# Rotary attention: statistics, root and normalizing of the next batch one quad of heads earlier; chunk attention: rows normalized by GpSimd

## The reference, cut to what matters

```python
x = x + _L0_attn_a_ref(_layernorm(x, axis=-1), Wq, Wk, Wv)          # "chunk attention"
x = x + _L0_ffn_ref(_layernorm(x, axis=-1), ...)                    # expert ffn
x = x + _L0_attn_b_ref(_layernorm(x, axis=-1), Wq, Wk, Wv, Wo, bo)  # "rotary attention"
...                                                                 # five more sublayers
```

## Time and profile before

| | |
|---|---|
| median of 3 runs | 4226.66 us (4223.68 to 4236.27) |
| the profiled execution | 4221.0 us, of which the span is 4219.3 us |
| TensorE busy | 3577.8 us (85%) |
| VectorE busy | 2677.2 us (63%) |
| ScalarE busy | 2302.2 us (55%) |
| GpSimd busy | 1990.1 us (47%) |
| mean granted TensorE clock | 0.907 of full speed |
| 500 to 600 us (chunk attention) | PE 95.71, DVE 86.40, ACT 70.01, POOL 25.44 of 100; granted clock 1.00 |
| 1600 to 2600 us (rotary attention) | PE 970.01, DVE 639.13, ACT 588.33, POOL 671.17 of 1000; granted clock 0.99 |

### The profile page before, as it was taken

One profiled execution on the slowest core, in us unless ns is written; L12 is line 12 of the kernel. 1 busy time (PEld: TensorE's weight loads), 2 busy tenths in 40 slices (PEclk: granted clock), 3 DMA queues, 4 the chain that ended last, 5 costly groups with the idle time before them and its releaser, 6 DMA issues. The chain is left out here.

```text
span 4219.3 us, 89135 instructions
## 1 busy us (share of the span) xinstructions
PE 3577.8 (85%) x31200; PEld 2222.9 (53%) x31295; DVE 2677.2 (63%) x5798; ACT 2302.2 (55%) x5504; POOL 1990.1 (47%) x1991
## 2 busy tenths in 40 slices
PE   5999999966858999999999999996857776787768
PEld 1333333325854556656565565555755665575546
DVE  6888888855445666666666666655455665555465
ACT  2766776753324556555555555553325553575367
POOL 2222222217435666666666666757431111565175
PEclk8999999985878999999999999995878997897879
DMA  5333333301551112111111111122542222110001
GB/s 98 58 58 58 58 58 58 58 28 59 184 160 45 47 41 50 42 44 48 42 47 44 41 47 45 44 54 60 182 145 63 68 65 50 33 62 6 1 1 41
DMA packets 418236, 252.24 MB, mean 60 GB/s; under 512 B 251186, under 2 KB 344354, under 8 KB 416642
## 3 DMA queue, kind: packets, MB, share of 16 engines
q1 hardware_dynamic: 409156, 228.56, 23.3%
q0 software_dynamic: 8640, 17.97, 1.3%
HBM read 75.12 MB, written 41.75 MB: 28 GB/s over the span
## 5 line engine op out<-in xcount | busy, mean ns | idle before, releaser
L2496 POOL TENSOR_TENSOR ra_prob<-ra_prob,ra_inverse 128x256 f32<-128x256 f32 (+3 forms) x512 | 630.6, 1253 | 472.0 <-DVE ra_inverse L2719 472.0
L2655 ACT ACTIVATE ra_prob<-ra_ps_s,ra_low 128x128 f32<-128x128 f32 (+3 forms) x1024 | 535.0, 530 | 320.6 <-DVE ra_low L2700 320.2
L2311 DVE TENSOR_REDUCE ca_mx<-ca_ps_s 128x2 f32<-128x1024 f32 x512 | 600.6, 1211 | 112.7 <-PE ca_ps_s L2172 112.4
L2237 ACT ACTIVATE ca_pT<-ca_ps_p 128x512 f32<-128x512 f32 x1024 | 548.8, 603 | 219.6 <-PE ca_ps_p L2182 195.0
L2700 DVE TENSOR_REDUCE ra_low<-ra_ps_s 128x2 f32<-128x256 f32 (+3 forms) x512 | 406.4, 815 | 77.5 <-PE ra_ps_s L2599 76.2
L2172 PE MATMUL ca_ps_s<-ca_kst,ca_qst 128*128 128x512 bf16 x991 | 381.2, 390 | 49.9 <-DVE ca_mx L2311 28.2
L2707 DVE TENSOR_TENSOR ra_prod<-ra_ps_r,ra_cos 128x512 f32<-128x512 f32 x256 | 176.6, 690 | 313.4 <-PE ra_ps_r L2561 265.2
L2182 PE MATMUL ca_ps_p<-ca_qst,ca_kst 128*128 128x512 bf16 x962 | 362.5, 382 | 4.9 <-ACT ca_pT L2237 4.5
L2536 PE MATMUL ra_ps_t<-ident,ra_prob 128*128 128x128 f32 x2560 | 352.9, 276 | 3.0 <-ACT ra_probT L2661 1.8
L2661 ACT COPY ra_probT<-ra_ps_t 128x512 f32<-128x512 f32 x384 | 226.4, 590 | 235.0 <-PE ra_ps_t L2536 234.9
L2489 POOL TENSOR_TENSOR ra_rot<-ra_prod 128x512 f32<-128x512 f32 x256 | 320.9, 1275 | 62.9 <-DVE ra_prod L2708 62.7
(11 more groups left out here) (413 smaller groups left out, 7162.2 us busy)
## 6 DMA issues: line engine op xcount, KB each, us to landing
moe_w_own<-moe_w1T SPq DMA_DIRECT2D x142, 256.0 KB
ra_qz<-ra_rot SPq DMA_DIRECT2D x512, 64.0 KB, 2.0
ra_kz<-ra_rot SPq DMA_DIRECT2D x512, 64.0 KB, 2.0
ca_kst<-ca_bounce SPq DMA_DIRECT2D x256, 64.0 KB
ca_bounce<-ca_thirds SPq DMA_DIRECT2D x192, 64.0 KB, 2.9
ca_qst<-ca_bounce SPq DMA_DIRECT2D x64, 192.0 KB
moe_hs<-moe_rows SPq DMA_DIRECT2D x142, 66.0 KB
moe_raw<-in_L_ffn_W SPq DMA_DIRECT2D x32, 256.0 KB, 3.2
```

Source lines behind the costliest of these rows:

```text
L2237: nc.scalar.activation(pT[:, (NS * hp + u) % PRING, :], ps_p[n % NP][:], ACT.Exp).then_inc(sg["drained"], 1)
L2311: nc.vector.tensor_reduce(mx[:, hm % 2, 2 * j:2 * j + 2], ps_s[m % 2][:].rearrange("p (b k) -> p b k", b=2), AX.X, ALU.max)\
L2496: nc.gpsimd.tensor_tensor(at, at, inverse[:, n % PROB, 2 * tile:2 * tile + 2].unsqueeze(2).broadcast_to([P, 2, keys]), ALU.mult)\
L2655: nc.scalar.activation(prob[:, n % PROB, tile, head, 0:keys], part(n, tile)[:, head, :], ACT.Exp, bias=low[:, n % PROB, at:at + 1], scale= ...
```

## The change

In chunk attention GpSimd applies the row norm to the two tiles itself, right behind the two roots, and VectorE's application at j = 12 is gone. VectorE's statistics now wait for the tile normalized two before, since the mean's buffer has two places. In rotary attention a new index `coming` marks the quad k = 4b - 2; statistics (slots 0 to 3) and root (slot 3) stand there, and the normalizing stands in its slot 7. The bias goes to slot 3 of quad 4b - 1; the transposes stay in slot 7 of that quad. The loop starts one iteration earlier (k = -2), in which only the norm of batch 0 stands.

```diff
@@ chunk_attention, gpsimd @@
                     if h is not None:
                         for c in range(2):
                             norm.rstd(pool, 2 * h + c, c)
+                        for c in range(2):
+                            t = 2 * h + c
+                            pool.wait_ge(norm.rstd_done, t + 1)
+                            nc.gpsimd.tensor_scalar(tile_of(xn, t), tile_of(X, t), norm.mv[:, c, 0:1], norm.rs[:, c:c + 1], ALU.subtract, ALU.mult)\
+                                .then_inc(sg["x_normed"], 1)
                     if hp is not None:
                         outputs(hp, 0)
@@ chunk_attention, vector @@
                         for c in range(2):
+                            wait(dve, sg["x_normed"], 2 * h + c - 1)
                             norm.stats(dve, 2 * h + c, c, tile_of(X, 2 * h + c))
-                    if j == 12:
-                        for c in range(2):
-                            dve.wait_ge(norm.rstd_done, 2 * h + c + 1)
-                            norm.apply(tile_of(xn, 2 * h + c), tile_of(X, 2 * h + c), c).then_inc(sg["x_normed"], 1)
@@ rope_attention, slots @@
-            for k in range(-1, QUADS + OUT):
+            for k in range(-2, QUADS + OUT):
...
-                    batch = (k + 1) // NQ if (k + 1) % NQ == 0 and k + 1 < QUADS else None
-                    body(j, t, s, front, score, value, out, batch)
+                    batch = (k + 1) // NQ if (k + 1) % NQ == 0 and 0 <= k + 1 < QUADS else None
+                    coming = (k + 2) // NQ if (k + 2) % NQ == 0 and k + 2 < QUADS else None
+                    body(j, t, s, front, score, value, out, batch, coming)
@@ rope_attention, gpsimd @@
+                    if coming is not None and j == 3:
+                        pool.wait_ge(sg["var_done"], coming + 1)
+                        nc.gpsimd.tensor_tensor(rs[:], var[:], core.minus_half[:, 0:TC], ALU.pow).then_inc(sg["rs_done"], 1)
+                    if coming is not None and j == 7:
+                        pool.wait_ge(sg["rs_done"], coming + 1)
+                        wait(pool, sg["x_turned"], coming)
+                        for c in range(TC):
+                            nc.gpsimd.tensor_scalar(xn[:, c, :], X[:, coming * TC + c, :], mv[:, c, 0:1], rs[:, c:c + 1], ALU.subtract, ALU.mult)\
+                                .then_inc(sg["x_normed"], 1)
                     if batch is not None and j == 3:
-                        pool.wait_ge(sg["var_done"], batch + 1)
-                        nc.gpsimd.tensor_tensor(rs[:], var[:], core.minus_half[:, 0:TC], ALU.pow).then_inc(sg["rs_done"], 1)
-                    if batch is not None and j == 5:
-                        ...
-                    if batch is not None and j == 7:
                         pool.wait_ge(sg["x_normed"], TC * (batch + 1))
                         xb = X[:, batch * TC:(batch + 1) * TC, :]
                         nc.gpsimd.tensor_tensor(xb, xb, bias[:].unsqueeze(1).broadcast_to([P, TC, D]), ALU.add).then_inc(sg["x_biased"], 1)
@@ rope_attention, vector @@
-                    if batch is not None and j < TC:
+                    if coming is not None and j < TC:
                         if j == 0:
-                            wait(dve, sg["x_normed"], TC * batch)
+                            wait(dve, sg["x_normed"], TC * coming)
...
```

More of the change, by code:

```diff
@@ L2462, in move, with body @@
                             sp.dma_start(to[at:at + HALF, n % RING, :], rot[h * HALF:(h + 1) * HALF, front % 2, o, x, :]).then_inc(qk_ready[n % RING], 16)
-                def body(j, t, s, front, score, value, out, batch):
+                def body(j, t, s, front, score, value, out, batch, coming):
                     if front is None or j not in (3, 5):
@@ L2507, in body @@
                         divide(score, 0)
-                    if batch is not None and j == 3:
-                        pool.wait_ge(sg["var_done"], batch + 1)
-                        nc.gpsimd.tensor_tensor(rs[:], var[:], core.minus_half[:, 0:TC], ALU.pow).then_inc(sg["rs_done"], 1)
-                    if batch is not None and j == 5:
[L2512 to L2516, removed]
-                    if batch is not None and j == 7:
+                    if coming is not None and j == 3:
[7 more added lines that the diff above has]
+                                .then_inc(sg["x_normed"], 1)
+                    if batch is not None and j == 3:
                         pool.wait_ge(sg["x_normed"], TC * (batch + 1))
@@ L2743, in body @@
                         minima(3, score)
-                    if batch is not None and j < TC:
+                    if coming is not None and j < TC:
                         if j == 0:
-                            wait(dve, sg["x_normed"], TC * batch)
-                        nc.vector.bn_stats(parts[:, j, :], X[:, batch * TC + j, :]).then_inc(sg["parts_done"], 1)
-                        dve.wait_ge(sg["parts_done"], TC * batch + j + 1)
+                            wait(dve, sg["x_normed"], TC * coming)
+                        nc.vector.bn_stats(parts[:, j, :], X[:, coming * TC + j, :]).then_inc(sg["parts_done"], 1)
+                        dve.wait_ge(sg["parts_done"], TC * coming + j + 1)
                         nc.vector.bn_aggr(mv[:, j, :], parts[:, j, :]).then_inc(sg["mean_done"], 1)
                         if j == TC - 1:
-                            dve.wait_ge(sg["mean_done"], TC * (batch + 1))
+                            dve.wait_ge(sg["mean_done"], TC * (coming + 1))
                             nc.vector.tensor_scalar(var[:], mv[:, :, 1], EPS, None, ALU.add).then_inc(sg["var_done"], 1)
```

## The result

The changed kernel takes 4157.27 us (median of 4 runs, 4155.79 to 4163.97) against 4229.05 us for the kernel before beside it (4223.68 to 4236.27): 71.8 us less, ratio 0.9832, 95% interval 0.9813 to 0.9851. The forecast was 4158. Measured again later it was 4142.74 against 4221.75, 79.0 us less, ratio 0.9816 (0.9799 to 0.9833).

What follows compares the result with a forecast made beforehand. TensorE's list was taken to bound rotary attention, with a stop for normalizing at each batch. Gains of 61.1 us there and 7.1 in chunk attention, 68.2 together, off the 4226.7 median gave 4158, range 4142 to 4178.

Steps and rivals of the forecast that it cites:

- clock, bias, waits and copy: Allowances: 5 us for the clock in other stages, 9 rotary bias, 6 chunk attention's VectorE waits, 15 ScalarE's rotary copy.
- The stop and the clock: Rotary attention: TensorE's 15 stops of 2.87 us, 43.0, and the slow clock behind them, 18.1, go: 61.1 us won.
- What is late next: Rotary slot 7: neither VectorE's bank nor ScalarE's copy stops TensorE; nothing taken, copy bounded at 15 us in all.
- The statistics: Rotary attention: the statistics' extra 0.61 us reappears a quad earlier, no change; up to 9 us won if absorbed.
- The 1.2 us for steps 2 and 3: Chunk attention: these steps are VectorE's own and gain 0.59 us each, 1.2 us together.
- The 1.2 us at the start: Chunk attention's start: GpSimd's slower first applications make everything behind them 1.2 us later.
- the 1.0 us for VectorE's new waits: Chunk attention: the second of two new waits per step costs a 0.03 us hand-over, 1 us in all.
- (1): Rotary batch boundary stays a stop through ScalarE's copy: 15 us, 18.1 more if the clock falls; 4173 to 4191, chance 0.08.
- (2): Chunk attention: GpSimd and VectorE block each other, 44 us on top, 4202; chance 0.05.
- (3): Rotary attention: normalizing delays the next division, 47 us plus 44 for the clock, 4250, slower than before; chance 0.02.
- (4): Rotary attention's wait stays and only chunk attention's 7 us are won, lost in noise: 4220 to 4227; chance 0.02.
- (5): More is won: rotary attention's 0.61 goes and chunk attention gives all of 16.5, so 4140; chance 0.05.

Runs made afterwards that it cites:

- the part alone: Under the stop and the clock: only the rotary attention change, against the kernel before; 4155.52 against 4217.01 us, ratio 0.9852.
- the run with 15 longer stops and 3 falls: Changed kernel with rotary attention's normalizing back in slot 5 and the bias in slot 7, statistics and root still early; 4195.65 us in one run.
- threefold normalizing: Changed kernel with GpSimd's slot 7 normalizing in rotary attention done three times, twice into a spare tile; 4151.81 us in one run.
- fourfold: Changed kernel with GpSimd's slot 7 normalizing in rotary attention done four times, three into a spare tile; 4197.44 us in one run.
- chunk part alone: Only the chunk attention change, against the kernel before; 4208.47 against 4217.01 us, ratio 0.9979.

## Why the prediction was right, point by point

**The number: closer than the forecast deserved.** 4158 against 4157.27 is partly luck. The forecast gain was 68.2 us, the measured ones are 71.8 and 79.0, and the kernel before, from which I subtracted, stood at 4229.05 beside the changed one instead of 4226.66. The range doesn't follow from its own terms either: clock, bias, waits and copy add up to 5 + 9 + 6 + 15 = 35 us upward, which is 4193 and not 4178, and the lower bound of -3 for chunk attention has no working.

**The stop and the clock: right.** Forecast 61.1 us. The stretch of rotary attention fell from 1571.8 to 1509.1, 62.7 us, and the part alone gave 61.5. The place of the normalizing was shown to be the cause by putting it back, which gave back 53.7 of the 62.7. The split of the forecast, 43.0 for the stops and 18.1 for the slow clock, describes the kernel before only: how often the clock falls behind such a stop is not given by the stops' length, as the run with 15 longer stops and 3 falls shows. The 18.1 us were read, not predicted; had the clock never fallen in the kernel before, the same edit would have given some 43 us.

**What is late next: right.** Nothing. The transposes' own cost was a little less than taken (23.37 - 22.79 = 0.58 instead of 0.66), which is 1.2 of the 1.6 us that the forecast lacks. ScalarE's copy is covered by 1.6 us. The bias behaves as costed: rotation without idle time, nobody waits.

**The statistics: right.** The 0.61 reappeared one quad earlier, at all batches: 1684.11 - 1660.71 is 23.40, and the next quad, which had it before, is 22.77. I gave its absence a small chance, and it needed an edit of its own to go. My reading of the cause was wrong in one link: the projection held by VectorE's multiplication idles for the same 0.76 us in plain quads (the earlier trace rows has 10.6 us in 14; the same row by "issue" has 33.4 us in 44), and the 0.61 us arise behind it, where VectorE's copy is late for the transposes of the probabilities.

**Chunk attention: right in sum, wrong in two terms.** Per steady step 0.33 us instead of 0.29, so about 9 instead of 8.1. The 1.2 us for steps 2 and 3 can't be told from the spread of the start: from the first to the fifth transposes it is 90.56 and 89.26 us where VectorE applies, and 85.7 to 89.8 in three profiles where GpSimd does. The 1.2 us at the start were a wrong term: the step that failed is "with everything behind it". I followed the chain through the engines and did not ask what the DMAs in it wait for; their landing hid the delay. And the 1.0 us for VectorE's new waits does not show: the eight rows of statistics take 1.51 to 1.52 us in a step as before, in all but two of 27 steps (1.66 and 1.68). The part alone gave 8.5 us against 7.1.

**The rivals.** (1) ScalarE's copy: it has 1.93 us of idle time before it instead of 5.33 and delays nobody. (2) GpSimd and VectorE in each other's way: no, 1211 ns a reduction in both kernels, and 1214 directly beside GpSimd's application. The Trainium skill, SBUF — State Buffer, section Who interferes with whom, which excludes a reduction from the port pair that the two engines share, agrees with that row. (3) The late division: it needs over 6 us more work on GpSimd than the change puts there; threefold normalizing costs almost nothing, fourfold 3.4 us a batch. (4) and (5) did not happen; further moves of the statistics won the 0.61 us a batch and 0.51 us a step.

**From profile to median.** The profiled executions differ by 62.8 us and the medians by 71.8 and 79.0. Chunk attention and rotary attention account for 8.3 and 62.7 in the profiles; the expert ffn between them was 4.5 us longer in the profile after and the stages behind rotary attention 3.7, and they are 3.8 and 9.9 us shorter again in the changed kernel's second profile. I had allowed 5 us for that; it is about twice as much from one execution to another. What sets it was not tried.

## What to carry to other kernels

Before moving work off a path, measure the repeating unit of the trace with and without the stop (here 26.3 and 22.79 us per quad): the difference, less what the work itself costs (0.6 us for the transposes) and with what a slow clock behind it adds, is the gain, and it needs no model of the engines. Before a wait is made the cause of such a difference, look whether the same row has the same idle time where the difference is absent. Work that a critical engine will need once per several units belongs in the last idle stretch of its own engine before them, not directly ahead of its use; how much fits there is the idle time plus what the next user can wait, which only a run with more work in it shows. And a chain that passes through a DMA is only as late as the DMA's landing: look there before carrying a delay on.

## What the runs showed of the hardware

- A stop of TensorE of about 3 us costs 0, about 1.6 or about 2.9 us more behind it, by a clock granted at half speed for some microseconds or not at all. The length of the stop alone does not decide which: with stops of 2.87 us every 96.6 us the clock fell 8 times in 15, with stops of 3.13 us it fell 3 times, and the last twelve of them, 95.54 us apart, were all without a fall. In the kernel before, the cost goes 2.9, 1.6, 0, 0 over every four stops; in the chunk part alone, where the same stops come some 12 us earlier, it is the same order.
- GpSimd's `tensor_scalar` on 128x128 float32 takes 0.79 to 0.80 us (VectorE 0.34), and 64 of them in chunk attention, where VectorE reduces meanwhile, took 794 to 819 ns each (chunk part alone). The reductions beside them took 1214 ns instead of 1211: neither engine slows the other there to speak of.
- In two executions of the same program the first scores, which wait for a DMA, start at 40.60 and 43.29 us, 2.7 us apart, though SP issued these DMAs at the same times to 0.1 us.
